# Attention maxima: the bias added by VectorE from a table in SBUF, in the instruction that takes the maximum

## The reference

```python
q = proj(wq, bq); k = proj(wk, bk); v = proj(wv, bv)           # x_seq @ w + b, by heads
scores = jnp.einsum('bhqd,bhkd->bhqk', q, k) / jnp.sqrt(jnp.float32(d_k))
scores = scores + _spatial_bias_matrix(spatial_bias, H, W)[None, None]
attn = jax.nn.softmax(scores, axis=-1)
ctx = jnp.einsum('bhqk,bhkd->bhqd', attn, v)
```

## Time and profile before

| | us |
|---|---|
| median of 3 runs | 14171.25 (14164.81 to 14183.32) |
| profiled execution | 14178.28 |
| span of its profile | 14176.7 |
| TensorE busy | 13118.8 (93%) |
| VectorE busy | 10007.6 (71%) |
| ScalarE busy | 6425.9 (45%) |
| GpSimd busy | 891.7 (6%) |

### The profile page before, as it was taken

How to read it: one execution, slowest core, us unless ns; L and a number is a source line. 1 busy time by engine, 2 the same in 40 slices (tenths; PEclk the granted TensorE clock), 3 DMA queues, 4 the chain that set the end, 5 groups by cost and what they waited for, 6 DMA issues and landing times.

```text
span 14176.7 us, 304054 instructions
## 1 busy us (share of the span) xinstructions
PE 13118.8 (93%) x110635; PEld 5455.4 (38%) x110635; DVE 10007.6 (71%) x17426; ACT 6425.9 (45%) x7576; POOL 891.7 (6%) x1062
## 2 busy tenths in 40 slices
PE   8888479999999999999999999999999999999999
PEld 4444123333333333333333333333333333333333
DVE  3555167777777777777777777777777777777776
ACT  1111025554555545554555455545555455545555
POOL 0222110001000000000000100000000000010000
PEclk8888569999999999999999999999999999999999
DMA  3443122222222222222222222222222222222121
GB/s 65 88 88 80 43 41 35 39 41 40 36 37 42 40 38 37 41 40 39 36 40 38 42 35 37 42 40 39 38 39 40 39 40 37 39 42 40 36 38 30
DMA packets 317569, 607.72 MB, mean 43 GB/s; under 512 B 63894, under 2 KB 248750, under 8 KB 315054
## 3 DMA queue, kind: packets, MB, share of 16 engines
q1 hardware_dynamic: 294618, 535.94, 20.8%
q0 software_dynamic: 21504, 51.47, 1.3%
HBM read 328.18 MB, written 53.47 MB: 27 GB/s over the span
## 4 chain that ended last, share of the span: by engine, by line
PE 71%; DVE 9%; issue 5%; ACT 2%; DVEq 0%; SPq 0%; DMA 0%; ACTq 0%; POOL 0%; POOLq 0%
PE l_ps L947 18%; PE l_ps L930 17%; PE l_ps L914 15%; PE l_ps L918 15%; DVE partial L1194 6%; PE l_ps L971 3%; PE l_ps L989 1%; PE l_ps L982 1%; ACT q_max L1089 1%; PE l_ps L975 1%; ACT p L1116 1%; DVE recip L1214 1%; DVE win_exp L1189 0%; DVE qs L1161 0%; DVE ks L1161 0%
## 5 line engine op out<-in xcount | busy, mean ns | idle before, releaser
L1194 DVE TENSOR_REDUCE partial<-l_ps 120x1 f32<-120x448 f32 x12544 | 7356.3, 621 | 2001.3 <-PE l_ps L947 1988.3
L1116 ACT ACTIVATE p<-l_ps 120x896 f32<-120x896 f32 x6272 | 5722.9, 917 | 5605.3 <-PE l_ps L918 5536.5
L947 PE MATMUL l_ps<-key_win,q_pick 128*56 128x448 f16 (+1 forms) x25088 | 4482.2, 365 | 407.4 <-DVE partial L1194 259.9
L914 PE MATMUL l_ps<-q_exp,ks 65*56 65x448 f16 (+1 forms) x25088 | 4543.4, 361 | 40.5 <-DVE win_exp L1189 27.7
L918 PE MATMUL l_ps<-win_exp,fold 112*56 112x448 f16 x25088 | 4513.8, 359 | 0.0
L930 PE MATMUL l_ps<-p,v 120*32 120x448 f32 x25088 | 3052.5, 559 | 2.1 <-ACT p L1116 2.1
L947 PEld LDWEIGHTS l_ps<-key_win,q_pick 128*64 128x64 f16 (+1 forms) x25088 | 1331.5, 108 | 3913.8 <-DVE partial L1194 3171.9
L914 PEld LDWEIGHTS l_ps<-q_exp,ks 65*64 65x64 f16 (+1 forms) x25088 | 1403.1, 110 | 1189.2 <-issue 282.6
L918 PEld LDWEIGHTS l_ps<-win_exp,fold 112*56 112x56 f16 x25088 | 1381.3, 109 | 924.3 <-issue 42.4
L930 PEld LDWEIGHTS l_ps<-p,v 120*32 120x32 f32 x25088 | 499.6, 109 | 1052.4 <-issue 1021.1
L866 POOL CAST half<-full 128x448 f16<-128x448 f32 x448 | 270.4, 604 | 5959.3 <-ACT full L1080 5959.3
(11 more groups left out here) (135 smaller groups left out, 5520.5 us busy)
## 6 DMA issues: line engine op xcount, KB each, us to landing
key_win<-ks SPq DMA_DIRECT2D x1792, 112.0 KB, 2.8
key_win<-by_query_scratch SPq DMA_DIRECT2D x224, 868.0 KB, 5.9
x<-in_x SPq DMA_DIRECT2D x16, 1568.0 KB
xc<-y_scratch POOLq DMA_DIRECT2D x224, 112.0 KB, 2.7
h_scratch<-x SPq DMA_DIRECT2D x8, 1568.0 KB
w_scratch<-x SPq DMA_DIRECT2D x8, 1568.0 KB
mh<-h_scratch SPq DMA_DIRECT2D x64, 196.0 KB
mw<-w_scratch SPq DMA_DIRECT2D x64, 196.0 KB
```

Source lines behind the costliest of these rows:

```text
L914: nc.tensor.matmul(ps[r * GP:r * GP + m, bank, 0:CH], ks[g][:, j, k0:k0 + m], q_exp[:, j, :], start=True, stop=True)
L947: last = nc.tensor.matmul(ps[r * GP:r * GP + wide, AB + i % 2, 0:CH], q_pick[:, j, q0:q0 + wide], rows(key_win[place][:])[:, s0:s0 + QC, 0 ...
L1116: nc.scalar.activation(p[k % 4][:], ps[0:GP + W, bank:bank + 2, 0:CH], ACT.Exp).then_inc(exp_done, 1)
L1194: nc.vector.tensor_reduce(partial[:, tile, kc:kc + 1], ps[0:GP + W, AB + i % 2, 0:CH], AX.X, ALU.max).then_inc(max_done, 1)
```

## The change

The matmuls of the maximum pass compute q times k alone: stationary is `q_pick`, now with the 65 partitions of the scores' operands, and moving are the keys `ks[g]` themselves, which lie in SBUF already. VectorE adds the bias: `tensor_tensor_reduce` adds the PSUM tile and a slice of `query_win` in SBUF, writes the sum to `scores_sum` in f16 and its maximum to `partial`. `query_win` is copied once per chunk by `stage_max` from `by_query`, which is loaded once into SBUF by two more loads at the end of the setup. `key_win`, its loads by SP and the waits for them go.

```diff
-STG_Q = (H + QC - 2) * RP
+STG_Q = (H + QC - 2) * W
+LOWEST = -3.0e38
...
-        q_pick = sb("q_pick", [128, HG, CH], F16)
-
-        key_win = [sb(f"key_win{i}", [DK + KT, STG_Q], F16) for i in range(2)]
+        q_pick = sb("q_pick", [STK + 1, HG, CH], F16)
+        by_query, query_win = sb("by_query_sb", [GP + W, (DIAG - 1) * W], F16), sb("query_win", [GP + W, STG_Q], F16)
+        scores_sum = sb("scores_sum", [GP + W, 2, CH], F16)
...
-            sp.wait_ge(clear, CLEARED)
-            with sp.Fori(0, B) as b:
-                for g in range(NG):
-                    G = b * NG + g
-                    with sp.Fori(0, NC) as c:
-                        for i in range(UT * HG):
-                            u, j = i // HG, i % HG
-
-                            sp.wait_ge(score_ready, ((G * NC + c) * UT * HG + i - 1) * NC + AHEAD)
-                            sp.sem_inc(passed, 1)
-                            if i < 2:
-                                sp.dma_start(key_win[i][DK:DK + KT, :],
-                                             scr["by_query"][:, bass.ds((H - QC - c * QC) * RP, STG_Q)]).then_inc(win_in[i], 16)
-                                sp.wait_ge(proj_done, (G + 1) * PJ)
-                                sp.sem_inc(passed, 1)
-                            s0 = (QC - 2 - 2 * u) * RP
-                            sp.dma_start(key_win[i % 2][0:DK, s0:s0 + H * RP], ks[g][0:DK, j, :]).then_inc(keys_in[i % 2], 16)
+            for r in range(2):
+                load(rows(by_query[r * GP:r * GP + W, :], W), rows(scr["by_query"][r * W:(r + 1) * W, :])[:, :, 0:W])
...
-            def max_scores(m, i):
+            def max_scores(m, g, i):
 
                 tile, kc = i // NC, i % NC
-                u, j, place = tile // HG, tile % HG, tile % 2
-                if i in (0, NC):
-                    pe.wait_ge(win_in[place], (m + 1) * 16)
-                if kc == 0:
-                    pe.wait_ge(keys_in[place], (m * UT * HG // 2 + tile // 2 + 1) * 16)
+                u, j = tile // HG, tile % HG
                 if i >= 2:
                     pe.wait_ge(max_done, m * MX + i - 1)
-                s0 = QC * kc - 2 * u + QC - 2
                 for r, wide in enumerate((GP, W)):
                     q0 = u * KT + r * W
                     last = nc.tensor.matmul(ps[r * GP:r * GP + wide, AB + i % 2, 0:CH], q_pick[:, j, q0:q0 + wide],
-                                            rows(key_win[place][:])[:, s0:s0 + QC, 0:W], start=True, stop=True)
+                                            rows(ks[g][:, j, :])[:, kc * QC:(kc + 1) * QC, 0:W], start=True, stop=True)
                 last.then_inc(score_ready, 1)
...
+            nc.vector.memset(by_query[:], 0.0)
...
-            nc.vector.tensor_copy(q_pick[:].rearrange("p h (u q) -> p (h u) q", q=KT),
-                                  w["ident"][:, DK:DK + KT].unsqueeze(1).broadcast_to([128, HG * UT, KT]))
+            nc.vector.memset(q_pick[STK:STK + 1], 0.0)
...
             def stage_max(m, c):
                 dve.wait_ge(staged_exp, HEAD + m * 2)
                 nc.vector.tensor_copy(q_max[0:STK], qs[:, :, bass.ds(c * CH, CH)]).then_inc(staged_max, 1)
+                dve.wait_ge(max_done, m * MX)
+                dve.sem_inc(passed, 1)
+                nc.vector.tensor_copy(query_win[:], by_query[:, bass.ds((H - QC) * W - c * (QC * W), STG_Q)]).then_inc(staged_win, 1)
...
-            def find_max(i, base):
+            def find_max(i, base, m):
                 tile, kc = i // NC, i % NC
+                s0 = QC * kc - 2 * (tile // HG) + QC - 2
+                if i == 0:
+                    dve.wait_ge(staged_win, m + 1)
                 dve.wait_ge(score_ready, AHEAD + base + i + 1)
-                nc.vector.tensor_reduce(partial[:, tile, kc:kc + 1], ps[0:GP + W, AB + i % 2, 0:CH], AX.X,
-                                        ALU.max).then_inc(max_done, 1)
+                if i >= 2:
+                    dve.wait_ge(max_done, base + i - 1)
+                dve.sem_inc(passed, 1)
+                nc.vector.tensor_tensor_reduce(scores_sum[:, i % 2, :], ps[0:GP + W, AB + i % 2, 0:CH],
+                                               query_win[:, s0 * W:(s0 + QC) * W], 1.0, LOWEST, ALU.add, ALU.max,
+                                               partial[:, tile, kc:kc + 1]).then_inc(max_done, 1)
```

More of the change, by code:

```diff
@@ L722, in layer1 @@
         staged_max, staged_pick, staged_exp = sem("staged_max"), sem("staged_pick"), sem("staged_exp")
-        win_in, keys_in = [sem(f"win_in{i}") for i in range(2)], [sem(f"keys_in{i}") for i in range(2)]
+        staged_win = sem("staged_win")
         score_ready, max_done, neg_ready, row_copied = sem("score_ready"), sem("max_done"), sem("neg_ready"), sem("row_copied")
@@ L734, in layer1 @@
         PJ = NC * 4
-        LOADS = 8 + 16 + 1 + HEADS + 2 + 3 + 2
+        LOADS = 8 + 16 + 1 + HEADS + 2 + 3 + 2 + 2
         K_CTX, K_SUM, K_RECIP, K_MIX, K_NORM = 2, 3, 5, 10, 11
@@ L1002, in _ @@
                 for i in range(MX):
-                    max_scores(z, i)
+                    max_scores(z, 0, i)
                 turn_rows(z, z + PREP)
@@ L1021, in next_max @@
                                 if i is not None:
-                                    max_scores(m, i)
+                                    max_scores(m, 1 - g if isinstance(c, int) and c == NC - 1 else g, i)
                             if k % 2 == 0:
@@ L1182, in stage_pick @@
                 dve.sem_inc(passed, 1)
-                nc.vector.tensor_copy(q_pick[0:DK], qs[0:DK, :, bass.ds(c * CH, CH)]).then_inc(staged_pick, 1)
+                nc.vector.tensor_copy(q_pick[0:STK], qs[:, :, bass.ds(c * CH, CH)]).then_inc(staged_pick, 1)
             def stage_exp(n, c):
@@ L1309, in _ @@
                 stage_max(z, z)
-                nc.vector.tensor_copy(q_pick[0:DK], qs[0:DK, :, 0:CH]).then_inc(staged_pick, 1)
+                nc.vector.tensor_copy(q_pick[0:STK], qs[:, :, 0:CH]).then_inc(staged_pick, 1)
                 for i in range(MX):
-                    find_max(i, z)
+                    find_max(i, z, z)
                 join_max(z)
@@ L1338, in step @@
                                 for i in range(ahead(k - 1, g, c), ahead(k, g, c)):
-                                    find_max(i, m * MX)
+                                    find_max(i, m * MX, m)
                                 if k == K_ROWS - 3:
```

## The result

| | before | after |
|---|---|---|
| median of 4 runs, us | 14177.3 (14164.8 to 14191.6) | 16873.8 (16709.5 to 16980.3) |
| profiled execution, us (its span) | 14178.3 (14176.7) | 16709.5 (16707.9) |
| mean granted TensorE clock | 0.949 | 0.813 |
| maxima on VectorE: busy us, mean ns | 7356.3, 621 | 7580.2, 623, and 1040.2, 83 |

The change makes the kernel slower by the ratio 1.187 (95% interval 1.179 to 1.195), which leaves out the run of 16980.3, 1.6% above the fastest. Between the medians of all runs it is 2696 us, where 563 were forecast. The result lies above the whole range that was given. Most of the loss is TensorE at half its clock.

The account below looks back on a forecast made before the run. TensorE was taken as the bound, leaning on VectorE. Per chunk 2.5 + 2.0 + 0.3 = 4.8 us, 533 for 111 chunks; with 7 + 28 it is 568, so 14740 us, 4% slower; range 14450 to 15100.

Parts of the forecast that it names:

- the last sentence on what goes: Score matmuls keep their 448 columns and the copy to q_pick its 1792 elements per partition, so both keep their time.
- First instruction: VectorE's add-and-max over 448 columns, once per tile: 0.62 us, bounds 0.62 and 0.68.
- Second instruction: VectorE's 120x1 write behind each add-and-max: releases the PSUM bank 0.08 us later, pitch per tile 0.61 us.
- The wait in front: Register operation ahead of the pair that carries the wait for the score in most tiles: 0.04 us.
- The pair together: Both VectorE instructions per tile: 2.5 us per chunk in plain sub-steps plus 2.0 in VectorE-bound ones.
- The copy: Table copy to query_win between q_max and a chunk's first tile: 0.3 us per chunk, bounds 0 and 1.07.
- Once: Costs outside the chunk loop: 7 us for 112 tiles running alone before it, 28 us of setup.
- Serial pairs: Rival: the two VectorE instructions don't overlap, 0.78 to 0.84 us per tile; some 15400 to 16100 us, chance 0.17.
- half rate: Rival: the add-and-max needs two passes of the 448 columns, 1.08 us per tile; some 18750 us, chance 0.04.
- hidden: Rival: the second instruction costs nothing in the loop and slack takes the register operation; 14240 us, chance 0.12.
- faster: Rival: 47 waits at the score line come from late key loads or slowed code fetch and go; 14130 us, chance 0.05.
- several times the 249: Sign that the forecast is right: TensorE's wait for VectorE at its score line grows to several times 249 us.

Follow-up runs that it names:

- pad128: The changed kernel with ks and q_pick filled up from 65 to 128 partitions, ones against zeros; 14741.9 us, ratio 1.038 to the kernel before.
- late_release: two_waits with a small memset behind each maximum that carries the release of the PSUM bank; 14478.3 us, ratio 1.021.
- two_waits: The kernel before with one more, always finished, wait per maximum and the increment of `passed`, ahead of TENSOR_REDUCE; 14468.2 us, ratio 1.021.
- no_transfers: pad128 with plain TENSOR_REDUCE and without the table copy, so the kernel before without the key_win loads; 14215.0 us, ratio 1.002.
- before_ttr: The kernel before, transfers and 128 rows kept, with the add-and-max pair adding zeros in place of TENSOR_REDUCE; 14586.8 us, ratio 1.028.
- experiment 8: pad128 with 96 partitions in place of 128, followed by a table of clock falls per version; 14994.5 us, ratio 1.057.

## Why the prediction was wrong

**The step that failed** is the last sentence on what goes: "The score matmuls keep their 448 columns ... so both keep their time". At a given clock they do: the pair of 128 rows shows 0.35 to 0.38 us, and one of 65 rows in the same timeline of before

```profile
6039.93 0.35 PE L914 MATMUL l_ps<-q_exp,ks 65*64 65x448 f16 x2
```

The clock is what they did not keep. The 65 partitions were listed as part of the change and costed at nothing, and no rival held a change of clock. What the runs showed in its place: with 65 rows the mean clock is 0.813, and each fall of the clock lasts 45 us where it lasts 7. That step hid 2132 of the 2696 us, as pad128 shows by the rows alone.

The Trainium skill (TensorE: Matmul & The Clock Gate, "The HAM clock gate") ties the granted clock to how busy TensorE has been. By that, a stretch without idle time should run at the full clock. The rows above disagree: 20.00 of 20 us busy, at 0.50. By the same page of the Trainium skill ("Why this matters for your kernels") a matmul of few rows takes the time of one of 128; the trace agrees (0.35 us for the pair of 65 rows, 0.35 to 0.38 for that of 128) only as long as the clock is the same.

The prediction also set its rows against a rule of the Trainium skill (VectorE: DVE Perf Modes, "The DRAIN you can't avoid"), that the next VectorE operation waits for an empty pipe. That section of the Trainium skill adds that a next operation which is not held starts earlier, so an overlap of 0.08 us in those rows doesn't contradict it. No number of the forecast rests on this.

**What the rest was.** pad128 came out at 14742, and the forecast was 14740. That is partly luck, since its terms were off in both directions (568 us forecast in all, 540 measured against 14202.0 in the runs beside pad128):
- *First instruction*: 0.62 forecast, 0.62 measured.
- *Second instruction*: a release 0.08 later forecast, 0.01 measured; late_release prices it at nothing. The pitch is 0.55 at best, not 0.61.
- *The wait in front*: 0.04 forecast, from a register operation's own 40 ns. Measured: 0.15 more from a score's start to its maximum's in two_waits, where TensorE and VectorE take turns, and 288 us in all. The row gave how long another operation lasts. The one in front of every maximum is the increment of `passed`, 50 ns. If it stands in full behind the wait, some 0.10 is left for an instruction whose wait is no longer its own; wait and increment were not tried apart.
- *The pair together*: 4.5 per chunk forecast (500 us), 385 measured, 3.5 per chunk.
- *The copy*: 0.3 per chunk forecast, 0.8 to 1.0 measured, near its upper bound of 1.07.
- *The transfers*: nothing forecast, nothing measured. The waits of 2.4 us for issue stayed, and new ones came: at the exponential's score line TensorE's waits for issue are 3 us in before, 25 in no_transfers and 43 in pad128 (2200 to 14000 us). Their cause is open.
- *Once*: 35 forecast. VectorE's last projection ahead of the first maximum pass starts 16 us later than before (1909.11 to 1925.28, below), and the pass itself is 10 us longer in before_ttr (7 forecast). no_transfers, with the setup but without the pair, is 33 above before; the other 17 are within the width of that interval (28 us), and the new waits for issue can hold most of them.

```profile
1909.11 1.37 DVE L1161 SCALAR_TENSOR_TENSOR ks<-half,flags_sb,full 64x448 f16<-64x448 f16 x2
```

```profile
1925.28 1.37 DVE L1143 SCALAR_TENSOR_TENSOR ks<-half,flags_sb,full 64x448 f16<-64x448 f16 x2
```

At 128 rows the parts nearly add up: 385 for the pair, 90 to 112 for the copy and 33 for the setup are 508 to 530, and pad128 stands 540 above before. At 65 rows they are worth more: 544 for the copy's place and 916 for the pair. The table behind experiment 8 shows why: without either there are fewer falls, and each fall lasts some 50 us.

**The rivals.** Serial pairs and half rate are out (pitch 0.55, first instruction 0.62), as are hidden and faster. The measured time lies beyond the first and short of the second, for a reason that none named.

**Its signs.** TensorE's waits at its score line from 2200 to 14000 us (total, times, longest), in the changed kernel and then in pad128:

```profile
PE l_ps L929 <- DVE partial L1185: 313.5, 545, 7.1
PE l_ps L929 <- issue: 81.6, 39, 2.4
```

```profile
PE l_ps L929 <- DVE partial L1185: 404.5, 794, 6.5
```

Neither is "several times the 249", so that sign was set wrong: at half clock VectorE is mostly ahead, and at full clock the wait is 1.6 times as long. That covers 155 us of pad128's 540; the rest shows in other waits or in none. A busy share of TensorE below 91% was to bear the forecast out (it is 91% in pad128); in the changed kernel it stayed at 93%, as if the kernel had not been slowed, since busy time counts a matmul at half clock as work. The clock row was the one to list.

## What to carry to other kernels

Where a change shrinks the partitions that matmuls contract over, count the granted clock as a term: compare its row before and after, and try filling the operands up to 128, one with zeros and the other with ones, which costs a few rows of memsets. In this kernel the rows decided how long a fall of the clock lasted, so one that stalls TensorE regularly is the first to try it on; no other kernel was tried here. And count a wait that is moved off its instruction at what its start loses (0.15 us here, with an increment), not at the register operation's own length.

## What the runs showed of the hardware

- TensorE ran for 100 us without idle time at 1.2 GHz with 65 rows in its score matmuls; with 63 rows of zeros against ones beside them it spent 7 us there per fall (pad128), where the changed kernel spent 45. The time went by degrees (16874, 14995, 14742 us at 65, 96 and 128 rows), and either kind of score matmul would do.
- What makes the clock return at 65 rows stays open. In the chunk above it came back in the midst of like work, and the rows ahead of it (TensorE's timeline of the changed kernel) show nothing different:

```profile
6162.85 0.59 PE L929 MATMUL l_ps<-ks,q_pick 65*56 65x448 f16 x2
6163.37 1.69 PE L917 MATMUL l_ps<-p,v 120*32 120x448 f32 x8
6164.99 0.57 PE L929 MATMUL l_ps<-ks,q_pick 65*64 65x448 f16 x4
6165.39 0.35 PE L901 MATMUL l_ps<-q_exp,ks 65*64 65x448 f16 x2
6165.58 0.35 PE L905 MATMUL l_ps<-win_exp,fold 112*56 112x448 f16 x2
```

- Whether the number of rows counts, or something that goes with it, was not separated: rows of other data than ones and zeros weren't tried.
- The same version varied more when its clock wandered: 16709 to 16980 in 4 runs of the changed kernel, 14732 to 14756 in 4 of pad128.
- An accumulator's read (83 ns) overlaps the end of its main instruction and the start of the next. Its price by itself was not measured; a memset of 59 ns in its place (late_release) cost nothing that the runs can tell.
